# Experts of a mixture of experts: rows turned by VectorE instead of TensorE, four upward banks, downward products three chunks behind

## The chip, the cores and the metric

The kernel runs on one core of a Trainium2 chip. The metric is device time in microseconds (us) of one execution: before the change 3318.99 us, the median of three runs (3316.73 to 3319.85).

## The reference

`x` is [8, 1024, 256], 8192 tokens of width 256. The block is a "macaron":

```
x = x + 0.5 * moe(layernorm(x))
x = x + rwkv6_attention(layernorm(x))
x = x + 0.5 * moe(layernorm(x))          # same expert weights

moe: logits = x @ router_w.T + router_b;  top 2 of 16 experts;  gates = softmax
     each expert takes at most 1280 of its tokens, in order; the rest is dropped
     h   = gelu(packed @ w1[e] + b1[e])     # 1280x256 @ 256x1024
     out = h @ w2[e] + b2[e]                # 1280x1024 @ 1024x256
     every token gets the gated sum of its experts' rows
```

The change touches the two expert stages alone (the line `h`, the line `out` and the gated sum).

## The kernel before, in words

Five stages run one after the other: constants, route a, experts a, attention with the second routing, experts b. A routing stage scatters each token's row into `slots` in DRAM, 260 floats a row: 256 of data and 4 of "tail" (token number, expert of its first choice, two gates). The stage `experts` (from L442) then takes the 16 experts in order.

One expert is 3 blocks of rows, `SIZES` = 512, 512 and 256 (L455). A block is 8 chunks (`FC`), a chunk being 128 of the 1024 hidden features; so an expert has 24 chunks, `c` counts them on, and `b`, `f` below are block and chunk in the block. A unit is 256 rows: units 0, 1 are block 0, units 2, 3 block 1, unit 4 block 2. All products are in three passes of a high and a low part (fp32r), so every operand is split: high by a cast, low by a subtraction.

The engines work through lists written out by hand, in order, and meet at semaphores:

- SP (`sp`, L539) loads weights in four parts per expert through two staging tiles, the rows of each unit (`load`, L547, one DMA of 256 runs of 1040 bytes) and the bias.
- TensorE (`pe`, L597): `up(c)` is 6 matmuls into a bank `pH` and `down(c)` is 4 pairs of matmuls (2 pairs in block 2) into `pO`, accumulated over the 8 chunks of a block. The loop (L659) does `up(c)`, then `down(c - LAG)`, with `LAG` = 2. After chunks f = 2 and 4 it turns one unit of the next block into `pT` (`turn`, L598, four 128x128 transposes). `up(c)` waits until the activations of `c - 2` have emptied its bank (two banks). `down` of the first chunk of a block waits until VectorE has taken the previous block's results out of the banks that it will overwrite (`out_ready`, L646).
- ScalarE (L677): two Gelu activations of each chunk, one into `h32`, one rounded into `hT` high.
- VectorE (L780): `split_h(c)` (L807) makes the low part of the activations; `out(m)` (L814) takes a unit's result out of `pO` in two instructions and signals `out_ready`; `split_x(m)` (L786) takes the turned rows out of `pT` into high and low parts, then gates and token numbers; `weights_low` makes the low part of a quarter of the next expert's weights. In the loop (L848) `out` of both units of the last block stands at f = 1, ahead of `split_h`; `split_x` stands at f = 3 and 5; `weights_low` at block 0, f = 4 and 7 and block 1, f = 4 and 7.
- GpSimd (L695): `weights_high` and, for each unit, `send`: scale by the gates and two indirect accumulating DMAs into `acc`. In stage b the last expert is added by VectorE instead (`fetch`, `merge`, `write`).

Of the kernel before, what the change touches and what calls it, by code (L numbers as in the profile page):

```python
# [6 lines left out]
U32 = mybir.dt.uint32  # L7
# [4 lines left out]
P = 128  # L12
# [429 lines left out]
def experts(nc, S, tag):  # L442

    with ExitStack() as ctx:
# [15 lines left out]
        LAG = 2  # L460
# [6 lines left out]
        xp = [sb(f"xp{m}", [P, 2, ROW]) for m in range(UNITS)]  # L467
# [16 lines left out]
        xp_loaded = [sem(f"xp_loaded{m}") for m in range(UNITS)]  # L484
# [22 lines left out]
        xp_d = S.slots[tag].rearrange("(n q p) d -> n p q d", p=P, q=2)  # L507
# [29 lines left out]
        with nc.Block() as block:  # L537
            @block.sync
            def _(sp):  # L539
                def weights(i, u, k):  # L540
                    if due(part(i, u, k)):
                        sp.wait_ge(w_split[k % 2], part(i, u, k))
                    e = i * 2 + u
                    src = w1_d[e][:, k, :] if k < 2 else w2_d[e][:, (k - 2) * 4:(k - 1) * 4, :]
                    sp.dma_start(staged(k), src).then_inc(w_loaded[k % 2], 16)

                def load(i, u, m):  # L547
                    n = i * NU + (u * UNITS + m)
                    if due(n - UNITS + 1):
                        sp.wait_ge(xp_free, n - UNITS + 1)  # L550
                    sp.dma_start(xp[m][:, :, :], xp_d[n]).then_inc(xp_loaded[m], 16)
# [8 lines left out]
                for m in range(2):  # L560
                    load(0, 0, m)
                for k in range(2, 4):
                    weights(0, 0, k)
                for m in range(2, UNITS):
                    load(0, 0, m)
                bias(0, 0)
                for m in range(2):
                    load(0, 1, m)

                def step(i, first, last):  # L570
                    for u in range(2):
                        if not (last and u == 1):
                            i1, u1 = (i, 1) if u == 0 else (i + 1, 0)
                            weights(i1, u1, 0)
                            bias(i1, u1)
                            for m in units(1):
                                load(i1, u1, m)
                            weights(i1, u1, 1)
                            weights(i1, u1, 2)
                            for m in units(2):  # L580
                                load(i1, u1, m)
                            weights(i1, u1, 3)
                        if not last:
                            for m in units(0):
                                load(i + 1, u, m)

                loop_with_ends(sp, E // 2, step)
                if END:
                    for m in range(UNITS):
                        sp.wait_ge(stored[m], (E - 1) * 32)  # L590
                    n = T // PARTS
                    for j in range(PARTS):
                        sp.dma_start(S.out[j * n:(j + 1) * n, :], S.acc[tag][j * n:(j + 1) * n, :]).then_inc(copied, 16)
                    sp.wait_ge(copied, PARTS * 16)

            @block.tensor
            def _(pe):  # L597
                def turn(i, u, m):  # L598
                    n = u * UNITS + m
                    pe.wait_ge(xp_loaded[m], i * 32 + (u * 16 + 16))  # L600
                    if due(i * NU + n - 1):
                        pe.wait_ge(xT_ready, i * NU + n - 1)
                    for q in range(2):
                        for k in range(DC):
                            t = pe.transpose(pT[n % 2][:, k, q * P:(q + 1) * P], xp[m][:, q, k * P:(k + 1) * P],  # L605
                                             S.ident[:, :])
                    t.then_inc(turned, 1)

                passes = [(HI, HI), (HI, LO), (LO, HI)]

                def up(i, c):
                    u, b, f = place(c)
                    if f == 0:
                        pe.wait_ge(xT_ready, i * NU + (u * UNITS + units(b)[-1] + 1))
                        if b == 0:
                            for k in range(2):
                                pe.wait_ge(w_split[k], part(i, u, k) + 1)
                    if due(i * NCH + c - 1):
                        pe.wait_ge(gelu_done, i * NCH + c - 1)
                    n = 0  # L620
                    for k in range(DC):
                        for a, z in passes:
                            t = pe.matmul(pH[c % 2][:, 0:SIZES[b]], w1[u][a][:, k, f * P:(f + 1) * P],  # L623
                                          xT[(u * BLOCKS + b) % 2][z][:, k, 0:SIZES[b]],
                                          start=(n == 0), stop=(n == 3 * DC - 1))
                            n += 1
                    t.then_inc(up_full, 1)

                def emptied(u, b, j):

                    m = 2 * b + j
                    if b == 0:
                        return u * UNITS - 1 - j
                    return u * UNITS + m - 2

                def down(i, c):
# [7 lines left out]
                    for q in range(SIZES[b] // P):  # L644
# [3 lines left out]
                        pe.matmul(pO[:, q, :], hT[s][HI][:, ts], w2[u][:, f, :, :].rearrange("p s d -> p (s d)"),  # L648
                                  start=(f == 0), stop=(f == FC - 1), skip_group_check=True)
                        t = pe.matmul(pO[:, q, 0:D], hT[s][LO][:, ts], w2[u][:, f, HI, :],  # L650
# [4 lines left out]

                for m in units(0):
                    turn(0, 0, m)

                def step(i, first, last):  # L659
                    for c in range(NCH):  # L660
# [4 lines left out]
                        u1, b1, over = after(u, b)  # L665
                        if f in (2, 4) and not (over and last):
                            j = f // 2 - 1
                            if j < len(units(b1)):
                                turn(i + 1 if over else i, u1, units(b1)[j])
# [7 lines left out]
            def _(act):  # L677
                def step(i, first, last):
                    for c in range(NCH):
# [7 lines left out]
                        for dst in (h32[c % 2], hT[c % SLOTS][HI]):  # L687
                            t = act.activation(dst[:, 0:SIZES[b]], pH[c % 2][:, 0:SIZES[b]], ACT.Gelu,  # L688
                                               bias=S.b1[:, bass.ds(i * (2 * FC) + (u * FC + f), 1)])
# [5 lines left out]
            def _(pool):  # L695
# [47 lines left out]
                def step(i, first, last):  # L743
                    for u in range(2):
# [10 lines left out]
                        more = not (last and u == 1)  # L755
                        if not (first and u == 0):
                            send(i if u else i - 1, 1 - u, UNITS - 1)
                        if more:
                            if due(i * NCH + u * CH):
                                pool.wait_ge(chunk_down, i * NCH + u * CH)  # L760
                            for k in range(2):
# [3 lines left out]
                        if more:  # L765
                            for k in range(2, 4):
                                weights_high(i1, u1, k)
# [12 lines left out]
            def _(dve):  # L780
# [5 lines left out]
                def split_x(i, u, m):  # L786
# [3 lines left out]
                    ts = slice(m % 2 * BS, m % 2 * BS + BS)  # L790
                    dve.wait_ge(turned, i * NU + n + 1)
# [4 lines left out]
                    dve.tensor_tensor(xT[r][LO][:, :, ts], pT[n % 2][:, :, :], xT[r][HI][:, :, ts],  # L796
                                      ALU.subtract).then_inc(xT_ready, 1)
                    if due(n + i * NU - UNITS + 1):
                        dve.wait_ge(stored[m], i * 64 + u * 32)
                    dve.scalar_tensor_tensor(out=gate[m][:, :], in0=xp[m][:, :, FIRST],  # L800
                                             scalar=S.iota_f[:, bass.ds(i * 2 + u, 1)], in1=xp[m][:, :, GATE01],
                                             op0=ALU.is_equal, op1=ALU.mult).then_inc(gate_part, 1)
                    dve.tensor_copy(to[m][:, :], xp[m][:, :, TOKEN].bitcast(U32))
                    dve.wait_ge(gate_part, i * NU + n + 1)
                    dve.tensor_tensor(gate[m][:, :], gate[m][:, :], xp[m][:, :, GATE1], ALU.add).then_inc(xp_free, 1)
# [8 lines left out]
                def out(i, u, m):  # L814
# [10 lines left out]
                    banks = slice(2 * (m % 2), 2 * (m % 2) + 2)  # L825
                    dve.tensor_tensor(ob[m][:, :, :], pO[:, banks, D:2 * D],  # L826
                                      b2[u][:, :].unsqueeze(1).to_broadcast([P, 2, D]), ALU.add).then_inc(out_part, 1)
                    dve.wait_ge(out_part, n + 1)
                    dve.tensor_tensor(ob[m][:, :, :], pO[:, banks, 0:D], ob[m][:, :, :],  # L829
# [17 lines left out]

                def step(i, first, last):  # L848
                    for c in range(NCH):
                        u, b, f = place(c)  # L850
                        if f == 1 and not (first and c < FC):
                            u0, b0, _ = place(c - FC)
                            for m in units(b0):
# [3 lines left out]
                        split_h(i, c)  # L857
# [5 lines left out]
                        if b < 2 and f in (4, 7) and not (last and u == 1):  # L863
                            weights_low(i if u == 0 else i + 1, 1 - u, 2 * b + f // 7)
# [1269 lines left out]
```

## Time and profile before

| | |
|---|---|
| median of three runs | 3318.99 us |
| the profiled execution | 3325.69 us, its span 3323.9 us |
| TensorE matmuls busy over the span | 2899.8 us, 87% |
| VectorE, ScalarE, GpSimd busy | 60%, 40%, 51% |
| experts a, experts b (first to last own instruction) | 295.7 to 1289.6 us, 2309.8 to 3316.3 us |
| DMA queue of SP, share of 16 engines | 20.3% |

A timeline row gives start, duration, engine, line, operation, output <- inputs, and in brackets how long the engine had been idle and what ended it. PE is TensorE's matmuls, DVE VectorE, ACT ScalarE, POOL GpSimd, SPq the sync engine's queue. A matmul's listed duration overlaps the next one's; its cost on the engine is the distance from its start to the next start.

### The profile page before, as it was taken

The numbers are of one execution on the slowest core, as the hardware profiler recorded it, in microseconds if no ns is written. First come the engines' busy times: TensorE is split into PE (matmuls) and PEld (weight loads), VectorE is DVE, ScalarE is ACT, GpSimd is POOL, SyncE is SP. The second block draws the span as 40 slices with busy tenths as digits, with TensorE's granted clock in tenths as the row PEclk, the third lists the DMA queues.
The fourth block names the chain that finished last, engine by engine and source line by source line (L and its number), as shares of the span: only waits on it lengthen the run. The fifth ranks groups of instructions, "written<-read, shape, count | busy, mean of one in ns | idle before, by whom it ended". The sixth has DMA issues, their size and how long they took to land. (4 is left out here: it accounts for less than half of the span.)

```text
span 3323.9 us, 63196 instructions
## 1 busy us (share of the span) xinstructions
PE 2899.8 (87%) x22656; PEld 2337.1 (70%) x22656; DVE 2005.2 (60%) x4425; ACT 1337.9 (40%) x2281; POOL 1695.3 (51%) x1510
## 2 busy tenths in 40 slices
PE   4453999999999995899999999974999999999997
PEld 4453888888888883466756666664888888888886
DVE  4343555555555653577888888753555555565563
ACT  3341444444444442343444444421444444444442
POOL 2543554554545443356676767644345445454543
PEclk9999999999999997899999999965999999999998
DMA  9813333343333324601111111002333334334334
GB/s 305 285 67 103 75 81 81 74 86 78 76 83 87 77 51 115 208 15 37 35 48 34 47 34 47 27 31 94 78 76 82 81 73 86 84 72 88 81 66 136
DMA packets 231849, 281.02 MB, mean 85 GB/s; under 512 B 18999, under 2 KB 214651, under 8 KB 231520
## 3 DMA queue, kind: packets, MB, share of 16 engines
q1 hardware_dynamic: 173760, 203.16, 20.3%
q0 software_dynamic: 57888, 75.16, 12.9%
q8 instruction: 130, 2.13, 0.3%
q14 instruction: 71, 0.58, 0.1%
HBM read 142.44 MB, written 146.41 MB: 87 GB/s over the span
## 5 line engine op out<-in xcount | busy, mean ns | idle before, releaser
L688 ACT ACTIVATE be_h<-be_pH,b 128x512 f32<-128x512 f32 (+1 forms) x384 | 237.2, 618 | 555.5 <-PE be_pH L623 483.1
L688 ACT ACTIVATE ae_h<-ae_pH,b 128x512 f32<-128x512 f32 (+1 forms) x384 | 237.2, 618 | 539.8 <-PE ae_pH L623 487.8
L714 POOL DMA_INDIRECT acc_a<-ae_ob,ae_to x160 | 254.9, 1593 | 94.1 <-POOL ae_ob L706 66.7
L706 POOL TENSOR_SCALAR ae_ob<-ae_ob,ae_gate 128x256 f32<-128x256 f32 x160 | 174.3, 1191 | 247.5 <-DVE ae_ob L829 247.5
L714 POOL DMA_INDIRECT acc_b<-be_ob,be_to x150 | 238.4, 1589 | 88.2 <-POOL be_ob L706 62.3
L706 POOL TENSOR_SCALAR be_ob<-be_ob,be_gate 128x256 f32<-128x256 f32 x150 | 163.0, 1183 | 222.4 <-DVE be_ob L829 222.4
L1461 POOL TENSOR_TENSOR m_xf<-m_tmp,m_xT 128x512 f32<-128x512 f32 x160 | 181.3, 1159 | 119.3 <-DVE m_tmp L1182 119.1
L434 POOL DMA_INDIRECT slots_a<-ar_row,ar_sidx x128 | 125.9, 984 | 158.7 <-issue 150.3
L1514 POOL DMA_INDIRECT slots_b<-m_row,m_sidx x128 | 152.9, 1195 | 84.0 <-issue 84.0
L1756 PEld LDWEIGHTS m_PP<-m_RP,m_KS 64*64 64x64 f32 x6656 | 121.1, 139 | 88.4 <-issue 87.3
L1756 PE MATMUL m_PP<-m_RP,m_KS 64*64 64x64 f32 x6656 | 135.7, 226 | 37.6 <-DVE m_A L1212 36.5
L811 DVE TENSOR_TENSOR ae_hT3l<-ae_h,ae_hT3h 128x512 fp32r<-128x512 f32 (+1 forms) x96 | 58.1, 605 | 162.1 <-ACT ae_hT3h L688 160.5
L811 DVE TENSOR_TENSOR be_hT3l<-be_h,be_hT3h 128x512 fp32r<-128x512 f32 (+1 forms) x96 | 58.1, 605 | 159.7 <-ACT be_hT3h L688 158.2
L1225 DVE TENSOR_TENSOR m_RP<-m_RP,m_tot 128x512 f32<-128x512 f32 x96 | 95.6, 996 | 80.9 <-PE m_PP L1756 80.9
L648 PE MATMUL be_pO<-be_w,be_hT1h 128*128 128x512 f32 x320 | 119.9, 405 | 22.2 <-DVE be_hT1l L811 22.2
L1182 DVE SCALAR_TENSOR_TENSOR m_tmp<-m_B,m_ch,m_xx 128x512 f32<-128x512 f32 x160 | 112.0, 741 | 44.6 <-PE m_B L1846 37.2
L648 PE MATMUL ae_pO<-ae_w,ae_hT1h 128*128 128x512 f32 x320 | 118.7, 402 | 16.3 <-DVE ae_hT1l L811 16.2
L648 PE MATMUL be_pO<-be_w,be_hT0h 128*128 128x512 f32 x320 | 122.5, 411 | 11.9 <-DVE be_ob L829 10.9
L648 PE MATMUL ae_pO<-ae_w,ae_hT0h 128*128 128x512 f32 x320 | 121.9, 409 | 8.3 <-DVE ae_ob L829 7.4
L648 PE MATMUL be_pO<-be_w,be_hT2h 128*128 128x512 f32 x320 | 117.6, 397 | 0.0
L648 PE MATMUL be_pO<-be_w,be_hT3h 128*128 128x512 f32 x320 | 117.0, 396 | 0.2 <-DVE be_hT3l L811 0.2
L648 PE MATMUL ae_pO<-ae_w,ae_hT3h 128*128 128x512 f32 x320 | 116.9, 396 | 0.2 <-DVE ae_hT3l L811 0.2
(342 smaller groups left out, 9384.7 us busy)
## 6 DMA issues: line engine op xcount, KB each, us to landing
ae_stage<-in_w SPq DMA_DIRECT2D x64, 512.0 KB
be_stage<-in_w SPq DMA_DIRECT2D x64, 512.0 KB
slots_a<-empty SPq DMA_DIRECT2D x10, 2080.0 KB, 19.7
ae_xp<-slots_a SPq DMA_DIRECT2D x80, 260.0 KB
slots_b<-empty SPq DMA_DIRECT2D x10, 2080.0 KB, 19.2
be_xp<-slots_b SPq DMA_DIRECT2D x80, 260.0 KB
ar_xin<-in_x SPq DMA_DIRECT2D x16, 512.0 KB, 5.8
acc_a<-ar_xin SPq DMA_DIRECT2D x16, 512.0 KB
```

The lines of the kernel that those rows point to most:

```text
L434: pool.indirect_dma_start(S.slots[tag][:, :], bass.IndirectOffsetOnAxis(ap=sidx[u][:, q, k:k + 1], axis=0), row[u][:, q, :], None, bounds_ ...
L648: pe.matmul(pO[:, q, :], hT[s][HI][:, ts], w2[u][:, f, :, :].rearrange("p s d -> p (s d)"), start=(f == 0), stop=(f == FC - 1), skip_group ...
L688: t = act.activation(dst[:, 0:SIZES[b]], pH[c % 2][:, 0:SIZES[b]], ACT.Gelu, bias=S.b1[:, bass.ds(i * (2 * FC) + (u * FC + f), 1)])
L706: t = pool.tensor_scalar(ob[m][:, q, :], ob[m][:, q, :], gate[m][:, q:q + 1], None, ALU.mult)
L714: pool.indirect_dma_start(S.acc[tag][:, :], bass.IndirectOffsetOnAxis(ap=to[m][:, q:q + 1], axis=0), ob[m][:, q, :], None, bounds_check=T ...
L811: dve.tensor_tensor(hT[s][LO][:, 0:SIZES[b]], h32[c % 2][:, 0:SIZES[b]], hT[s][HI][:, 0:SIZES[b]], ALU.subtract).then_inc(h_split, 1)
L1182: drains(dve.scalar_tensor_tensor(out=tmp[m % TMP][:, :], in0=bank(f"M{m}", g)[:, :], scalar=ch[:, 1 + f, k:k + 1], in1=xx[:, k, :], op0=A ...
L1225: dve.tensor_tensor(rp[:, :, 1, :], rp[:, :, 1, :], pieces(l)[:, :, 0:1].to_broadcast([P, DC * GT >> (l + 1), 1 << l]), ALU.mult).then_inc ...
L1461: pool.tensor_tensor(xf[f][:, k, :], tmp[m % TMP][:, :], xT[g % 2][:, k, 1:GT + 1], ALU.add).then_inc(mixed, 1)
L1514: pool.indirect_dma_start(S.slots["b"][:, :], bass.IndirectOffsetOnAxis(ap=sidx[w][:, q, k:k + 1], axis=0), row[w][:, q, :], None, bounds_ ...
L1756: t = pe.matmul(PP[c * N:c * N + N, h, to], ks[rows, r, ts], rp[rows, r, ss], start=True, stop=True, skip_group_check=True)
```

## The change

What it does, part by part:

1. TensorE's `turn` goes, and the banks `pT` with it. SP loads a block's rows so that each partition group j of 32 holds, for features 32j to 32j + 31 of each half, blocks of 32 rows by 32 features (`xq`): 8 DMAs per block, 24 per expert, of 128-byte runs. VectorE turns a unit with one `transpose` of 32x32 blocks (128x512) into `x32`, then casts and subtracts from there. The tails come by one DMA per expert.
2. `LAG` is 3, and `up` has four banks `pH`.
3. `pO` is two tiles of two banks. Units 0, 2, 4 have the first (`HOME` 0), units 1, 3 the second.
4. VectorE: `split_h` comes first in each step; `out` of the even unit at f = 2, of the odd one at f = 3, each behind `split_h` of that chunk. `weights_low` moves to block 0, f = 2, 4, 7 and block 1, f = 4.
5. SP issues both first weight parts of the next expert ahead of its rows; at the very start the rows of block 0 go first. GpSimd makes the next expert's first two high parts as soon as the last `up` of the expert before is done, ahead of `send` of its unit 4, and the other two right behind that `send`.

```diff
-        LAG = 2
+        LAG = 3
-        pT = [ps(f"pT{r}", [P, DC, BS]) for r in range(2)]
-        pH = [ps(f"pH{r}", [P, FULL]) for r in range(2)]
-        pO = ps("pO", [P, 4, 2 * D])
+        UPS = 4
+        pH = [ps(f"pH{r}", [P, FULL]) for r in range(UPS)]
+        pO = [ps(f"pO{r}", [P, 2, 2 * D]) for r in range(2)]
+        HOME = (0, 1, 0, 1, 0)
...
+                def load(i, u, b):
+                    m = units(b)[-1]
+                    if due(i * NU + (u - 1) * UNITS + m + 1):
+                        sp.wait_ge(xp_free, i * NU + ((u - 1) * UNITS + m + 1))
+                    e = i * 2 + u
+                    n0, n1 = b * FULL // BLK, (b * FULL + SIZES[b]) // BLK
+                    for j in range(QUADS):
+                        for k in range(DC):
+                            cs = slice(k * P + j * BLK, k * P + j * BLK + BLK)
+                            sp.dma_start(xq[b][j * BLK:(j + 1) * BLK, k, :].rearrange("i (n d) -> i n d", d=BLK),
+                                         x_d[e][:, n0:n1, cs]).then_inc(xq_loaded[b], 16)
...
+                load(0, 0, 0)
                 for k in range(2):
                     weights(0, 0, k)
...
-                            weights(i1, u1, 0)
+                            for k in range(2):
+                                weights(i1, u1, k)
+                            load(i1, u1, 0)
+                            load_tails(i1, u1)
                             bias(i1, u1)
...
+                            for k in range(2, 4):
+                                weights(i1, u1, k)
+                            load(i1, u1, 1)
+                            load(i1, u1, 2)
...
-                    if due(i * NCH + c - 1):
-                        pe.wait_ge(gelu_done, i * NCH + c - 1)
+                    if due(i * NCH + c - UPS + 1):
+                        pe.wait_ge(gelu_done, i * NCH + c - UPS + 1)
...
                     m = 2 * b + j
-                    if b == 0:
-                        return u * UNITS - 1 - j
-                    return u * UNITS + m - 2
+                    before = [k for k in range(m) if HOME[k] == HOME[m]]
+                    if before:
+                        return u * UNITS + before[-1]
+                    return (u - 1) * UNITS + [k for k in range(UNITS) if HOME[k] == HOME[m]][-1]
...
+                    dve.transpose(x32[n % 2][:, :, :], xq[b][:, :, ts]).then_inc(turned, 1)
                     dve.wait_ge(turned, i * NU + n + 1)
-                    dve.tensor_copy(xT[r][HI][:, :, ts], pT[n % 2][:, :, :]).then_inc(xT_high, 1)
+                    dve.tensor_copy(xT[r][HI][:, :, ts], x32[n % 2][:, :, :]).then_inc(xT_high, 1)
...
+                LOWS = [(0, 2), (0, 4), (0, 7), (1, 4)]
...
-                        if f == 1 and not (first and c < FC):
+                        split_h(i, c)
+                        if f in (2, 3) and not (first and c < FC):
                             u0, b0, _ = place(c - FC)
-                            for m in units(b0):
+                            for m in units(b0)[f - 2:f - 1]:
                                 out(i if c >= FC else i - 1, u0, m)
...
-                        split_h(i, c)
```

## Rows read from the trace of the kernel before

**Rows 1.** The page: granted clock in tenths and GB/s, in 40 slices.

```profile
PEclk9999999999999997899999999965999999999998
GB/s 305 285 67 103 75 81 81 74 86 78 76 83 87 77 51 115 208 15 37 35 48 34 47 34 47 27 31 94 78 76 82 81 73 86 84 72 88 81 66 136
```

**Rows 2.** Windows view, experts a: length, busy per engine (instructions), clock, DMA share, GB/s.

```profile
309.00:1281.00 972.00, 946.97 (x5164) 802.03 (x5164) 561.59 (x993) 430.50 (x766) 467.00 (x375) 1.00 0.36 76
```

**Rows 3.** Waits of TensorE, 309 to 1281: total us, times, longest.

```profile
PE ae_pO L648 <- DVE ae_hT1l L811: 16.2, 15, 1.7
PE ae_pO L648 <- DVE ae_ob L829: 7.4, 34, 0.3
PE ae_pH L623 <- ACT ae_hT0h L688: 0.4, 1, 0.4
```

**Rows 4.** Timeline, TensorE: the same place in two experts that follow each other.

```profile
532.37 0.50 PE L648 MATMUL ae_pO<-ae_w,ae_hT1h 128*128 128x512 f32 x1 [0.98 <-DVE ae_hT1l L811]
...
593.38 0.50 PE L648 MATMUL ae_pO<-ae_w,ae_hT1h 128*128 128x512 f32 x1 [0.98 <-DVE ae_hT1l L811]
```

**Rows 5.** Timeline at a change of block, 512-row chunks.

```profile
513.47 0.39 PE L623 MATMUL ae_pH<-ae_xT0h,ae_w_1l 128*128 128x512 f32 x1
513.70 0.40 PE L648 MATMUL ae_pO<-ae_w,ae_hT3h 128*128 128x512 f32 x1
...
513.99 0.69 ACT L688 ACTIVATE ae_h<-ae_pH,b 128x512 f32<-128x512 f32 x1 [1.53 <-PE ae_pH L623]
...
514.58 0.68 ACT L688 ACTIVATE ae_hT1h<-ae_pH,b 128x512 fp32r<-128x512 f32 x1
514.60 0.69 DVE L826 TENSOR_TENSOR ae_ob<-ae_pO,ae_b 128x512 f32<-128x512 f32 x1 [0.53 <-PE ae_pO L650]
...
515.11 0.40 PE L623 MATMUL ae_pH<-ae_xT0h,ae_w_1h 128*128 128x512 f32 x1
515.33 0.69 DVE L829 TENSOR_TENSOR ae_ob<-ae_pO,ae_ob 128x512 f32<-128x512 f32 x1
...
515.94 0.68 DVE L826 TENSOR_TENSOR ae_ob<-ae_pO,ae_b 128x512 f32<-128x512 f32 x1
...
517.39 0.50 PE L648 MATMUL ae_pO<-ae_w,ae_hT0h 128*128 128x512 f32 x1
```

**Rows 6.** Timeline in the 256-row block, with one turn and one `split_x`.

```profile
542.29 0.43 DVE L811 TENSOR_TENSOR ae_hT3l<-ae_h,ae_hT3h 128x256 fp32r<-128x256 f32 x1 [1.04 <-ACT ae_hT3h L688]
...
542.42 0.28 PE L623 MATMUL ae_pH<-ae_xT1h,ae_w_1l 128*128 128x256 f32 x1
...
542.63 0.68 DVE L794 CAST ae_xT0h<-ae_pT 128x512 fp32r<-128x512 f32 x1
...
542.83 0.48 ACT L688 ACTIVATE ae_h<-ae_pH,b 128x256 f32<-128x256 f32 x1 [0.57 <-PE ae_pH L623]
...
543.20 0.47 ACT L688 ACTIVATE ae_hT0h<-ae_pH,b 128x256 fp32r<-128x256 f32 x1
543.24 0.60 PE L605 MATMUL ae_pT<-ident,ae_xp 128*128 128x128 f32 x4
...
544.62 0.42 DVE L811 TENSOR_TENSOR ae_hT0l<-ae_h,ae_hT0h 128x256 fp32r<-128x256 f32 x1
```

**Rows 7.** Timeline, SP's queue at the start of experts a.

```profile
293.18 0.94 SPq L551 DMA_DIRECT2D ae_xp<-slots_a  x2
```

**Rows 8.** Waits of TensorE in the last expert of experts b, 3262 to 3302.

```profile
PE be_pO L648 <- DVE be_hT1l L811: 6.1, 2, 4.0
PE be_pO L648 <- DVE be_ob L829: 3.9, 2, 3.8
```

**Rows 9.** Windows view: behind the 2.0 us wait of rows 8, and around a 1.6 us wait.

```profile
3301.60:3304.90 3.30, 3.30 (x16) 3.11 (x15) 0.85 (x2) 0.84 (x2) 1.75 (x2) 0.50 0.33 119
2728.00:2732.00 4.00, 2.39 (x13) 1.67 (x12) 3.24 (x3) 1.06 (x2) 1.05 (x2) 1.00 0.16 25
```

**Rows 10.** DMA view, 1303.7 to 1305.1: strips of 128-byte runs loaded for attention.

```profile
DMA packets 1868, 0.28 MB, mean 202 GB/s; under 512 B 1792, under 2 KB 1868, under 8 KB 1868
```

More of the change, by code:

```diff
@@ L466, in experts @@
         b2 = [sb(f"b2_{u}", [P, D]) for u in range(2)]
-        xp = [sb(f"xp{m}", [P, 2, ROW]) for m in range(UNITS)]
+        xq = [sb(f"xq{b}", [P, DC, SIZES[b]]) for b in range(BLOCKS)]
+        tails = [sb(f"tails{u}", [P, 2 * UNITS, ROW - D]) for u in range(2)]
+        x32 = [sb(f"x32_{r}", [P, DC, BS]) for r in range(2)]
         xT = [[sb(f"xT{r}{k}", [P, DC, FULL], F32R) for k in "hl"] for r in range(2)]
@@ L483, in experts @@
         b2_loaded = [sem(f"b2_loaded{u}") for u in range(2)]
-        xp_loaded = [sem(f"xp_loaded{m}") for m in range(UNITS)]
+        xq_loaded = [sem(f"xq_loaded{b}") for b in range(BLOCKS)]
+        tails_loaded = [sem(f"tails_loaded{u}") for u in range(2)]
         stored = [sem(f"stored{m}") for m in range(UNITS)]
@@ L556, in bias @@
                     sp.dma_start(b2[u][:, :], S.b2[i * 2 + u].partition_broadcast(P)).then_inc(b2_loaded[u], 16)
+                load(0, 0, 0)
                 for k in range(2):
                     weights(0, 0, k)
[L560 to L561 removed]
+                load_tails(0, 0)
                 for k in range(2, 4):
                     weights(0, 0, k)
[L564 to L565 removed]
+                load(0, 0, 1)
                 bias(0, 0)
[L567 to L568 removed]
+                load(0, 0, 2)
                 def step(i, first, last):
@@ L597, in _ @@
             def _(pe):
[L598 to L607, printed above, removed]
                 passes = [(HI, HI), (HI, LO), (LO, HI)]
@@ L664, in step @@
                             down(i, c - LAG)
[L665 to L669, printed above, removed]
                     if last:
@@ L755, in step @@
                         more = not (last and u == 1)
+                        if more:
+                            if due(i * NCH + u * CH):
+                                pool.wait_ge(up_full, i * NCH + u * CH)
+                            for k in range(2):
+                                weights_high(i1, u1, k)
                         if not (first and u == 0):
@@ L760, in step @@
                                 pool.wait_ge(chunk_down, i * NCH + u * CH)
-                            for k in range(2):
+                            for k in range(2, 4):
                                 weights_high(i1, u1, k)
@@ L764, in step @@
                             send(i, u, m)
-                        if more:
-                            for k in range(2, 4):
-                                weights_high(i1, u1, k)
                         for m in units(1):
@@ L862, in step @@
                                 split_x(i + 1 if over else i, u1, units(b1)[j])
-                        if b < 2 and f in (4, 7) and not (last and u == 1):
-                            weights_low(i if u == 0 else i + 1, 1 - u, 2 * b + f // 7)
+                        if (b, f) in LOWS and not (last and u == 1):
+                            weights_low(i if u == 0 else i + 1, 1 - u, LOWS.index((b, f)))
                     if last:
```

57 lines of the change are left out of this document (27 added, 30 removed).

## The prediction

> **What bounds the kernel now.** I read the page first, then the windows of an expert stage, TensorE's waits, and last the timeline of one expert. The page's clock is at full speed in both expert stages [rows 1]. In experts a the matmuls are busy 947 of 972 us, VectorE 562, ScalarE 431, GpSimd 467 [rows 2]: TensorE is the bound, and only its own work or its own waits can move the time. Its waits are short: 16.2 us behind `split_h`, 7.4 us behind `out`, and 0.4 us in one wait for an upward bank [rows 3]. The last says that two more `pH` banks have nothing to remove by themselves.
>
> One expert lasts 61.01 us, the distance of the same matmul in two experts [rows 4]. Of that the products need: an `up` matmul 0.23 us, six are 1.40; a `down` of four pairs 513.70 to 515.11, 1.41 [rows 5]. A full chunk is 2.81 us, one of 256 rows half of it, 1.405. So 16 x 2.81 + 8 x 1.405 = 56.2 us. The other 4.8 us of each expert are five turns and the waits. That is all the change can take away: 32 experts x 4.8 = 154 us.
>
> **What goes.** All turns and, as the steps below put them elsewhere, all the old waits: -4.8 us an expert. The longest of these (0.98 us) stands in both experts at the same place, where `split_h` comes late [rows 4]; with `LAG` 3 `down(c)` runs one chunk later, 2.8 us more of slack, so that kind goes.
>
> **What comes: VectorE's `out` behind `split_h`.** This is the step that decides. `down(8)`, the first of block 1, overwrites the banks of units 0 and 1, so it needs `out(0)` for its first half and `out(1)` for its second. TensorE's order is now up(10), down(7), up(11), down(8). VectorE's is split_h(10), out(0), split_h(11), out(1). So `out(1)` cannot start before up(11) has gone through ScalarE and `split_h`, and down(8) stands right behind up(11). The length of that chain, from the start of the last `up` matmul: 0.52 to the first activation, 0.59 to the second, 0.68 for it, 0.61 for `split_h` (a VectorE instruction of this size frees the engine after 0.61, 515.33 to 515.94), 0.73 and 0.69 for the two of `out`, 0.03 to the matmul: 3.85 us [rows 5]. Without a wait TensorE would be there sooner. At each block change:
>
> - A, block 2 to the next expert's block 0: needs `out(4)`, behind split_h(f=2). TensorE comes after 0.23 + 0.70 (down, 256 rows) + 1.40 (up) = 2.34. Wait 1.51 us.
> - B, block 0 to 1: first half after 0.23 + 1.41 + 1.40 = 3.04, wait 0.81 for `out(0)`; second half, from up(11), after 0.23 + 0.71 = 0.94, so the two waits together are 3.85 - 0.94 = 2.91 us, the second 2.10.
> - C, block 1 to 2, 256-row chunks: the chain is 0.41 + 0.37 + 0.47 [rows 6] + 0.34 + 1.42 + 0.03 = 3.04, where 0.34 is 542.29 to 542.63. TensorE comes after 0.12 + 1.41 + 0.70 = 2.23. Wait 0.81 us.
>
> Before, both `out` stood at f = 1 ahead of `split_h`; those waits were at most 0.3 us [rows 3]. The chain has only latencies in it; while it runs nothing else on TensorE can go first.
>
> **D, the turned rows.** VectorE now also turns. The trace has no such instruction. The nearest row is the cast of the same 128x512 from `pT`: 0.68 us long, 0.72 to an instruction that waits for it, as between L826 and L829 (514.60 to 515.33) [rows 5]; I take 0.72. Below, it could be half, 0.36; above, 1.0. `split_x` took 542.63 to 544.62, 1.99 us [rows 6], and becomes 2.71. In block 2 two of them stand at f = 3 and 5 between short chunks. Counted from the last `up` matmul of f = 2: out(2) ends 2.93; split_h(f=3) waits for its activation and ends 3.70; out(3) 5.04; split_x(0) 7.75; two split_h 8.43; transpose, cast, subtraction: rows ready for TensorE at 8.43 + 0.72 + 0.72 + 0.72 = 10.59. TensorE, after the wait of C at 3.04, does down 0.81, then four ups and four downs, 5.64: it wants them at 9.48. Wait 1.1 us. With halves for transpose and cast it is 0; with 1.0 for the transpose 1.7.
>
> The Trainium skill says ("VectorE: DVE Perf Modes", section "The perf-mode tier table") that a one-source copy of fp32 from SBUF runs at twice the rate that a PSUM source allows. No row here has such a copy. By it the two casts of D would give back about 0.5 us an expert, 16 us in all, which stays inside the range.
>
> A matmul behind a wait lasts 0.50 instead of 0.40 [rows 4, 5]: five waits, 0.5 us. Sum an expert: 1.51 + 2.91 + 0.81 + 1.1 + 0.5 = 6.8 us new against 4.8 old, +2.0. Over 32 experts +65; A and D don't occur before a stage's first expert, -5.
>
> **Start of a stage.** Eight DMAs of rows stand ahead of the first weights. Two issues take 0.94 us [rows 7], so eight take 3.8, and the weights come that much later; two transposes add 1.4 before the first `up`. 2 x 5.2 = +10 us.
>
> **The last expert of stage b** waits twice, 3.8 and 4.0 us, for the fetched sums [rows 8]. `fetch` follows the send of unit 4, which is a chunk later now, but a late `merge` holds down(12) only three chunks on instead of two. I take half away: -4.
>
> **Clock.** After the wait of 2.0 us (the smaller of the 6.1 in two [rows 8]) TensorE ran at 1.2 GHz (granted 0.50) for 3.3 us; around a 1.6 us wait it stayed at 2.4 GHz (1.00) [rows 9]. B has 0.8 and 2.1 us within 4. If every B ended so, 3.3 us at half speed cost 1.65 us each, 32 x 1.65 = 53; if none, 0. B lies just beyond the row that fell; I take 30.
>
> **Costed at nothing.** SP has 30 issues an expert instead of 10, 30 x 0.47 = 14 of 61 us, and its waits are for buffers freed an expert earlier. Loads of the next rows are issued about 24 chunks before use. The 128-byte runs: 10,240 an expert. 1868 packets passed in 1.4 us [rows 10], 0.75 ns each, so 7.7 us an expert. `weights_high` has the time from the last `up` to f = 2. `weights_low` at f = 4 and 7 is covered by three chunks of lag; without the cover it would be the old wait of 1 us. GpSimd's and the DMA queues' order isn't on TensorE's path: TensorE never waited for weights [rows 3].
>
> **Sum**: +65 - 5 + 10 - 4 + 30 = +96 us. On the profiled execution 3325.7 + 96 = 3422; that execution was 6.7 us above the median, so on the median 3319 + 96 = 3415 us.
>
> **Rivals.**
>
> 1. Faster. The waits A to C don't bind: if VectorE reaches `out` before TensorE reaches the banks, as before, the 4.8 us of turns and waits go and only short waits as in rows 3 remain (0.3 x 4 an expert). Then -154 + 38 + 10 = about 3213 us. It decides where `out(1)` is ready within 0.94 us of the last `up` matmul of f = 3. For it: VectorE is idle 40% of the stage. Against: idle time does not help a list worked in order, and `split_h(11)` needs `up(11)`. Chance 0.08, and 0.03 more for half waits that cancel to within 0.2%.
> 2. Short runs make DMA the bound. At 0.75 ns this is far off. It decides from about 6 ns a packet. The Trainium skill says ("DMA: Bandwidth & Descriptors", section "Rules for kernel authors") that a plain DMA with a rearranged access pattern is 19 times slower than a hardware transpose. As a mechanism here: an expert's 1.33 MB at the page's best slice, 305 GB/s [rows 1], is 4.4 us; 19 times that is 83 us, more than the expert's 63. Then each expert lasts 83 us, +22 x 32: 4020 us. The strips of rows 10 are the same kind of run and passed at 202 GB/s, so 0.03.
> 3. The clock falls at every B, and the transpose takes 1.0 us: +23 and +17, 3455 us. Chance 0.12.
> 4. The change removes waits that are not there: "weights first" and the four banks. TensorE waited for neither, so this is part of my forecast.
>
> **Numbers.** Forecast as summed 0.74. Its own range: without D and without the clock -63, with rival 3 +40, and a few us for rounding: 3350 to 3458. This also holds 8 in 10 overall, since only rivals 1 and 2 lie outside. 0.2% (6.6 us) is about what a measurement of this kernel can tell from none. Faster 0.09, same 0.03, slower 0.88.
>
> **What would show it.** In the trace after: no L605; waits of `pO` matmuls for `ob` of 1.5, 0.8 + 2.1 and 0.8 us an expert, over 150 us in all; waits of `pH` matmuls for `xT` near 1 us; the period of an expert 63 to 64 us; stretches of granted clock 0.5 in the expert stages. I am wrong if the waits for `ob` stay near 0.3 us, if the period falls under 61, or if TensorE waits for `xq`.

## The result, and the profile after

The changed kernel takes 3484.5 us (median of 4, 3482.8 to 3487.4), the kernel before 3319.4 us (4 runs, 3316.7 to 3320.6): ratio 1.0498 [1.0484, 1.0513], 165 us slower. Forecast were 3415 us with a range to 3458. The direction was right, the size 70 us short.

The page of the changed kernel: busy times, granted clock in tenths, DMA packets.

```profile
PE 2901.2 (83%) x22016; PEld 2325.8 (67%) x22016; DVE 2132.3 (61%) x4585; ACT 1337.6 (38%) x2281; POOL 1783.2 (51%) x1510
PEclk9999999999999998799999999866999999999999
DMA packets 569771, 281.06 MB, mean 81 GB/s; under 512 B 397879, under 2 KB 552571, under 8 KB 569440
```

The windows view from the first `up` of experts a to their last matmul, before and after (columns as in [rows 2]):

```profile
303.20:1280.80 977.60, 952.39 (x5176) 805.99 (x5176) 564.23 (x997) 433.27 (x769) 467.85 (x376) 1.00 0.36 77
301.30:1365.60 1064.30, 957.22 (x4864) 802.97 (x4864) 631.87 (x1075) 433.11 (x769) 510.23 (x375) 0.96 0.40 70
```

TensorE executes fewer matmuls (x4864 against x5176, the turns are gone), is busy 5 us longer all the same, and the stage is 87 us longer; the clock over the stage is 0.96 where it was 1.00. So it waits, and part of its work runs slower. The profiled executions (3325.7 us before, 3487.4 after) differ by 161.7 us:

| Stretch | before | after | difference |
|---|---|---|---|
| up to SP's first issue of experts a | 292.3 | 283.5 | -8.9 |
| from there to the first `up` | 10.9 | 17.9 | +7.0 |
| first `up` to last matmul, experts a | 977.6 | 1064.3 | +86.6 |
| between the two expert stages | 1025.6 | 1029.4 | +3.7 |
| start of experts b | 10.9 | 18.2 | +7.3 |
| first `up` to last matmul, experts b | 993.3 | 1059.3 | +65.9 |

The first row is work that the change does not touch, and I leave it unexplained. The bodies hold 152.5 of the 161.7 us. The period of one expert went from 61.05 to 66.6 us; forecast were 63.0 and about 1 for the clock.

TensorE's waits, 312 to 1370 (total us, times, longest), the answer to [rows 3]:

```profile
PE ae_pO L653 <- DVE ae_ob L834: 93.6, 63, 3.0
PE ae_pH L626 <- DVE ae_xT1l L800: 7.4, 8, 1.0
PE ae_pH L626 <- DVE ae_xT0l L800: 6.0, 7, 1.0
```

The 16.2 us behind `split_h` are gone, as forecast. The 7.4 us behind `out` (34 times, at most 0.3) became 93.6 us, up to 3.0 each, and the turned rows cost 13.4. Sorted by place over both stages, all from the timeline:

| Wait | times | us in all | each | forecast each |
|---|---|---|---|---|
| A, next expert's block 0 | 30 | 81.8 | 2.73 | 1.51 |
| B, block 1, two waits | 32 pairs | 84.6 | 0.71 + 1.82 | 0.81 + 2.10 |
| C, block 2 | 32 | 23.5 | 0.7 | 0.81 |
| D, turned rows | 30 | 27 | 0.9 | 1.1 |

B, C and D are as predicted within 0.4 us. A is not.

The timeline of the changed kernel at an A and at the B behind it (start, length, engine and line, idle time before it in brackets), and the order of VectorE at each:

```profile
571.07 3.26 DVE L817 TENSOR_TENSOR ae_hT1l<-ae_h,ae_hT1h 128x512 fp32r<-128x512 f32 x1 [1.41 <-issue]
571.17 2.60 POOL L696 CAST ae_w_1h<-ae_stage 128x1024 fp32r<-128x1024 f32 x2
...
572.42 0.68 ACT L685 ACTIVATE ae_hT2h<-ae_pH,b 128x512 fp32r<-128x512 f32 x1
...
574.25 0.68 DVE L817 TENSOR_TENSOR ae_hT2l<-ae_h,ae_hT2h 128x512 fp32r<-128x512 f32 x1
574.85 0.68 DVE L831 TENSOR_TENSOR ae_ob<-ae_pO,ae_b 128x512 f32<-128x512 f32 x1
575.57 0.69 DVE L834 TENSOR_TENSOR ae_ob<-ae_pO,ae_ob 128x512 f32<-128x512 f32 x1
576.40 0.47 PE L653 MATMUL ae_pO<-ae_w,ae_hT0h 128*128 128x512 f32 x1 [2.69 <-DVE ae_ob L834]
...
597.58 0.69 DVE L817 TENSOR_TENSOR ae_hT2l<-ae_h,ae_hT2h 128x512 fp32r<-128x512 f32 x1 [2.09 <-ACT ae_hT2h L685]
...
599.65 0.50 PE L653 MATMUL ae_pO<-ae_w,ae_hT0h 128*128 128x512 f32 x1 [0.71 <-DVE ae_ob L834]
600.37 0.69 DVE L817 TENSOR_TENSOR ae_hT3l<-ae_h,ae_hT3h 128x512 fp32r<-128x512 f32 x1 [0.78 <-ACT ae_hT3h L685]
600.98 0.68 DVE L831 TENSOR_TENSOR ae_ob<-ae_pO,ae_b 128x512 f32<-128x512 f32 x1
...
602.30 0.70 DVE L794 STREAM_TRANSPOSE ae_x<-ae_xq 128x512 f32<-128x512 f32 x1
602.44 0.55 PE L653 MATMUL ae_pO<-ae_w,ae_hT0h 128*128 128x512 f32 x1 [1.82 <-DVE ae_ob L834]
603.04 0.43 DVE L798 CAST ae_xT0h<-ae_x 128x512 fp32r<-128x512 f32 x1
604.07 0.63 PE L626 MATMUL ae_pH<-ae_xT1l,ae_w_0h 128*128 128x512 f32 x1
604.50 0.63 PE L626 MATMUL ae_pH<-ae_xT1h,ae_w_0l 128*128 128x512 f32 x1
```

B is the forecast chain: `out` stands behind a `split_h` that waits for its activation. At A, `split_h` of f = 1 lasts 3.26 us instead of 0.69. It runs beside GpSimd's first two casts of the next weights, 571.17 to 573.77, which the change moved there, and ends 0.56 us after the second. The activation that `split_h` of f = 2 needs ends at 573.10, but `split_h` starts only at 574.25: 1.15 us late, and the wait is 2.69 instead of 1.51, 1.18 more. In the whole trace 28 of the 512 `split_h` of this width overlap both casts of a pair and last 3.26 to 3.58 us; all 67 that overlap a cast average 2.26 us, and of the other 445, with a mean of 0.69, none lasts over 0.92. The Trainium skill states a mechanism ("SBUF — State Buffer", section "Who interferes with whom"): a VectorE instruction with two inputs in SBUF contends with a GpSimd instruction that reads SBUF. The trace agrees, with 0.69 against 2.26 us. But overlap alone is not enough: in `e10` below 91 `split_h` overlap a cast and average 0.82 us, none over 1.58. What makes the difference was not separated.

Behind B the matmuls of one product start 0.43 us apart, 604.07 to 604.50, not 0.23. The windows view of B's two waits and of the stretch behind them, the answer to [rows 9]:

```profile
596.00:602.70 6.70, 4.17 (x20) 3.02 (x19) 4.28 (x7) 2.54 (x4) 2.05 (x2) 1.00 0.00 0
602.80:606.10 3.30, 3.30 (x10) 2.72 (x9) 1.65 (x6) 0.00 (x0) 3.00 (x3) 0.50 0.39 42
```

TensorE goes from 2.4 GHz (1.00) to 1.2 GHz (0.50) behind the pair of waits. This happened behind 31 of the 32 B (109 us at 1.2 GHz) and behind 14 of the 30 A (58 us). Half of these 167 us, 83, is lost, since a matmul takes 0.43 us there and not 0.23.

The lines view of VectorE, 312 to 1370 (busy us, mean ns, idle before):

```profile
L817 DVE TENSOR_TENSOR ae_hT1l<-ae_h,ae_hT1h 128x512 fp32r<-128x512 f32 x63 | 90.4, 1434 | 88.7 <-ACT ae_hT1h L685 76.6 <-issue 12.1
L794 DVE STREAM_TRANSPOSE ae_x<-ae_xq 128x512 f32<-128x512 f32 x78 | 54.7, 702 | 0.0
L798 DVE CAST ae_xT1h<-ae_x 128x512 fp32r<-128x512 f32 x40 | 19.9, 498 | 1.4
```

The turn of 128x512 takes 0.70 us (0.72 was assumed). `split_h` into `hT1l`, the one beside the casts, has a mean of 1.43.

### The profile page after: what moved, and what is told of

It reads as the page before. It is cut to its first block and busy times, and to the rows that moved or that the text cites. A ratio compares the mean times of both kernels' runs of the same rounds, so it can differ in the third digit from the quotient of the medians.

```text
span 3485.6 us, 63656 instructions
## 1 busy us (share of the span) xinstructions
PE 2901.2 (83%) x22016; PEld 2325.8 (67%) x22016; DVE 2132.3 (61%) x4585; ACT 1337.6 (38%) x2281; POOL 1783.2 (51%) x1510
## 2 busy tenths in 40 slices
DMA packets 569771, 281.06 MB, mean 81 GB/s; under 512 B 397879, under 2 KB 552571, under 8 KB 569440
## 5 line engine op out<-in xcount | busy, mean ns | idle before, releaser
L703 POOL TENSOR_SCALAR ae_ob<-ae_ob,ae_gate 128x256 f32<-128x256 f32 x160 | 210.6, 1464 | 400.0 <-DVE ae_ob L834 400.0
L703 POOL TENSOR_SCALAR be_ob<-be_ob,be_gate 128x256 f32<-128x256 f32 x150 | 199.8, 1489 | 370.5 <-DVE be_ob L834 370.5
L653 PE MATMUL ae_pO<-ae_w,ae_hT0h 128*128 128x512 f32 x320 | 130.3, 433 | 93.6 <-DVE ae_ob L834 93.6
L1763 PEld LDWEIGHTS m_PP<-m_RP,m_KS 64*64 64x64 f32 x6656 | 121.4, 139 | 85.7 <-issue 84.6
L817 DVE TENSOR_TENSOR be_hT1l<-be_h,be_hT1h 128x512 fp32r<-128x512 f32 (+1 forms) x96 | 108.0, 1125 | 114.9 <-ACT be_hT1h L685 103.4
L817 DVE TENSOR_TENSOR ae_hT1l<-ae_h,ae_hT1h 128x512 fp32r<-128x512 f32 (+1 forms) x96 | 104.6, 1090 | 117.2 <-ACT ae_hT1h L685 105.1
L653 PEld LDWEIGHTS be_pO<-be_w,be_hT0h 128*128 128x128 f32 x320 | 62.2, 194 | 128.8 <-DVE be_ob L834 59.3
L817 DVE TENSOR_TENSOR ae_hT0l<-ae_h,ae_hT0h 128x512 fp32r<-128x512 f32 (+1 forms) x96 | 63.7, 664 | 136.5 <-ACT ae_hT0h L685 130.1
L653 PEld LDWEIGHTS ae_pO<-ae_w,ae_hT0h 128*128 128x128 f32 x320 | 62.8, 196 | 126.3 <-DVE ae_ob L834 58.5
L1232 DVE TENSOR_TENSOR m_RP<-m_RP,m_tot 128x512 f32<-128x512 f32 x96 | 85.4, 890 | 91.7 <-PE m_PP L1763 91.6
L817 DVE TENSOR_TENSOR be_hT0l<-be_h,be_hT0h 128x512 fp32r<-128x512 f32 (+1 forms) x96 | 58.2, 607 | 128.6 <-ACT be_hT0h L685 121.4
L626 PE MATMUL ae_pH<-ae_xT0h,ae_w_0h 128*128 128x512 f32 (+1 forms) x256 | 88.9, 347 | 55.4 <-DVE ae_xT0l L800 55.4
```

The source lines that it names most:

```text
L626: t = pe.matmul(pH[c % UPS][:, 0:SIZES[b]], w1[u][a][:, k, f * P:(f + 1) * P], xT[(u * BLOCKS + b) % 2][z][:, k, 0:SIZES[b]], start=(n == ...
L653: pe.matmul(to[:, q % 2, :], hT[s][HI][:, ts], w2[u][:, f, :, :].rearrange("p s d -> p (s d)"), start=(f == 0), stop=(f == FC - 1), skip_g ...
L703: t = pool.tensor_scalar(ob[m][:, q, :], ob[m][:, q, :], gate[m][:, q:q + 1], None, ALU.mult)
L817: dve.tensor_tensor(hT[s][LO][:, 0:SIZES[b]], h32[c % 2][:, 0:SIZES[b]], hT[s][HI][:, 0:SIZES[b]], ALU.subtract).then_inc(h_split, 1)
L1763: t = pe.matmul(PP[c * N:c * N + N, h, to], ks[rows, r, ts], rp[rows, r, ss], start=True, stop=True, skip_group_check=True)
```

## The experiments

Every kernel was timed in three rounds beside the kernel before, on the same chip. `e1`, `e3`, `e4` and `e5` ran where the kernel before took 3318.6 us; `e2`, `e6`, `e7` and `e8` ran on a second chip, where it took 3273.2 us, and `e9` to `e12` on a third, where it took 3272.4. So only ratios to the kernel before are compared, and a gain in us is such a ratio times 3319.

### e1: both `out` first

```diff
 # after, VectorE's list
-split_h(i, c)
-if f in (2, 3) and not (first and c < FC):
+if f == LAG - 1 and not (first and c < FC):
     u0, b0, _ = place(c - FC)
-    for m in units(b0)[f - 2:f - 1]:
+    for m in units(b0):
         out(i if c >= FC else i - 1, u0, m)
+split_h(i, c)
```

> The kernel after with one thing moved on VectorE: both out of the last block stand at f = 2 ahead of split_h, as before they stood at f = 1 with a lag of two. Theory 1 (the time was lost because out(1) stands behind split_h of a chunk whose up is right ahead of the down that needs it; the clock fell behind those waits): the waits of pO matmuls for ob shrink from about 190 us to under 20 us, the stretches at 1.2 GHz inside the expert stages (168 us) nearly go, an expert takes about 58 us in place of 66.5, and the time is 3200 to 3240 us, under the kernel before too. Rival (the loads in 128-byte runs or the transposes on VectorE cost the time): these stay, so it stays above 3400 us.

1.0050 [1.0032, 1.0067], 3333.3 us: it gives back most of the loss, but not what was expected. B's and C's waits are gone, so the order of `out` made them. A stays, 2.1 to 2.4 us in 28 of 30 places, with 75 us at 1.2 GHz behind it. The waits of TensorE for `ob` in `e1`, 312 to 1170:

```profile
PE ae_pO L653 <- DVE ae_ob L834: 28.9, 15, 2.4
```

Fifteen waits, one an expert at most. This is the part that order alone does not explain.

### e2: GpSimd's casts at their old places

```diff
 # after, GpSimd's step: send of unit 4, then casts 0 and 1; sends of block 0, then casts 2 and 3
-LOWS = [(0, 2), (0, 4), (0, 7), (1, 4)]
+LOWS = [(0, 4), (0, 7), (1, 4), (1, 7)]
```

> The kernel after with only GpSimd's casts and VectorE's weights_low back at their old places; out stays behind split_h. Theory: the wait at block 2 to 0 falls from 2.7 to the 1.5 us that the chain of latencies gives, the clock falls at block 0 to 1 alone: 30 x 1.2 plus half of the 58 us of slow clock behind it, 3484 - 65 = 3420 us. Rival (the casts do not matter): 3475 to 3490 us.

1.0389 [1.0372, 1.0406], which is 0.990 of the changed kernel's ratio, some 36 us, where 65 were expected. `out` stays behind `split_h`. A falls to 1.59 us in all 30 places, against the 1.51 of the forecast, and no `split_h` lasts over 1.5 us. B and C stay. So the early casts, and not the order of `out`, made the rest of A. At 1.2 GHz there are 65 us instead of 167: the same pair of waits at B now drops the clock 12 times of 32, not 31. But a wait of 1.4 us for `split_h` comes back at chunk 13 (block 1, f = 5, the place of [rows 4]), 19 times over the two stages, 28 us in all, the second group here (TensorE, 312 to 1170):

```profile
PE ae_pO L653 <- DVE ae_ob L832: 63.8, 53, 1.8
PE ae_pO L653 <- DVE ae_hT1l L815: 12.1, 8, 2.1
```

### e3: only the turning on VectorE and SP's order

`LAG` and `UPS` are 2, both `out` first, casts and `LOWS` as in `e2`.

> Rows by block turned by VectorE, and SP's new order, alone: lag 2, two upward banks, both out at f = 1 ahead of split_h, GpSimd's and weights_low's places as in the kernel before. Theory 1: TensorE's five turns (about 2.2 us an expert) go, a wait for the turned rows of under 1 us comes; 3250 to 3300 us. Rival (loads and transposes cost): at or above 3400 us, as the kernel after.

1.0099 [1.0081, 1.0117], against an expectation of no more than 0.995. TensorE's turns are gone, but the old wait for `split_h` at chunk 13 grew from 0.98 us [rows 4] to 2.1:

```profile
PE ae_pO L653 <- DVE ae_hT1l L815: 34.3, 26, 3.4
```

Just ahead of that `split_h` VectorE waits for a cast of GpSimd in `weights_low`, in the kernel before (L783) and in `e3` (L780):

```profile
529.68 2.03 DVE L783 TENSOR_TENSOR ae_w<-ae_stage,ae_w 128x1024 fp32r<-128x1024 f32 x1 [4.57 <-POOL ae_w L699]
530.79 2.04 DVE L780 TENSOR_TENSOR ae_w<-ae_stage,ae_w 128x1024 fp32r<-128x1024 f32 x1 [5.00 <-POOL ae_w L696]
```

So VectorE has time to spare there; it is GpSimd that comes 1.1 us later against TensorE's arrival. Its `send` ahead of the casts scales for 3.1 us where it took 2.4, and starts later. TensorE also waits 12 times in a stage, 0.5 us each, for one of its two upward banks.

### e4: only the order and the banks

The kernel before with `LAG` 3, four output banks by `HOME`, and `out` behind `split_h` at f = 2 and 3. TensorE turns.

> The kernel before with the order alone: lag 3, out of the even unit at f = 2 and of the odd one at f = 3, each behind split_h, pO in two homes; turns stay on TensorE, two upward banks, loads as before. Theory 1: the waits of 1.5 to 2.8, 0.7 + 1.8 and 0.7 us come as in the kernel after, and the clock falls behind them; about the kernel after plus the turns less the wait for turned rows: 3480 to 3540 us. Rival (loads and transposes cost): near the kernel before, 3300 to 3360 us.

1.0381 [1.0363, 1.0399], 3443.5 us. B is 0.34 + 2.43 us, C 0.34, A 1.13, and 120 us of the two stages run at 1.2 GHz. It came out below the expected 3480, but 125 us on the slow side, far from the rival: three quarters of the loss come without VectorE's turns. `e4` has no wait at chunk 13. Against `e9` below, which has the same lag with `out` first (1.0045), the order of `out` and its banks cost 3.3%, some 110 us.

### e5: keeping TensorE busy in its waits

```diff
 # after, before the waits of A and of B's second half; the products land in a free upward bank and are thrown away
+def fill(i, c):
+    pe.wait_ge(gelu_done, i * NCH + c - UPS + 1)
+    for r in range(FILL):        # 16
+        pe.transpose(pH[c % UPS][:, 0:P], S.ones[:, :], S.ident[:, :])
```

> The kernel after with 16 transposes of constants (about 1.75 us of TensorE work that is thrown away) ahead of two of its waits: down's second half at block 0 to 1 and down's first half at the next expert's block 0. If the clock falls because TensorE stands still there, the stretches at 1.2 GHz (92 and 76 us in the two expert stages) go, each giving back half its length: 84 us less, about 3400 us, while out_ready comes no earlier. If the clock is not what these waits cost, the time stays within 10 us of 3484 or rises by the filling.

1.0295 [1.0274, 1.0317], 3416.1 us, 68 us less than the changed kernel, with nothing else changed. No stretch at 1.2 GHz begins in the two stages. The windows view of experts a, clock 1.00 where it was 0.96:

```profile
303.00:1325.00 1022.00, 970.41 (x5360) 827.22 (x5360) 642.71 (x1075) 432.56 (x769) 525.20 (x375) 1.00 0.42 73
```

Of the 83 us that the clock cost, 68 came back. The chains behind the waits remain; the thrown-away products fill part of them (36 us of waiting for `ob` are left of experts a's 94). This measures the clock's term apart from the waits, rather too low than too high, since the filling adds work.

### e6: the same rows in long runs

```diff
 # after, SP's load of rows: as many DMAs and bytes; an expert's rows are other numbers
-x_d[e][:, n0:n1, cs]          # runs of 128 bytes
+xl_d[e][rows, units, 0:D]     # runs of 1024 bytes
```

> The kernel after with the rows loaded in 1024-byte runs in the same number of DMAs and bytes; VectorE turns what lies there, so the expert inputs are other numbers. If the 128-byte runs cost anything, the time falls from 3484 us by that; my theory says within 10 us of 3484 and the same waits of TensorE. Rival (the loads slow the stage): 50 us less or more.

Packets under 512 bytes fall from 397,879 to 70,196. 1.0512 [1.0492, 1.0531] against 1.0498 [1.0484, 1.0513]: the intervals overlap. No cost of the short runs shows, as forecast. The 19-fold rule of the Trainium skill ("DMA: Bandwidth & Descriptors", section "Rules for kernel authors") that the prediction weighed does not decide this kernel's time.

### e7 and e8: the casts later, then the rows earlier

```diff
 # e7 = e1 with the casts and LOWS of e2
 # e8 = e7 with this in VectorE's list
-if f in (3, 5) and not (over and last):
+turns = (1, 4) if b == BLOCKS - 1 else (3, 5)
+if f in turns and not (over and last):
```

> As the run with out first, and GpSimd's casts of the next weights' high parts and VectorE's weights_low back at their old places: casts behind send of unit 4, weights_low at block 0, f = 4, 7 and block 1, f = 4, 7. Theory: the wait of 2.1 to 2.7 us at block 2 to 0 is there because the two early casts on GpSimd (2.6 us) run beside split_h(f=1), which then takes 3.3 us in place of 0.7 and holds back split_h(f=2) and out(4). With them later that wait is about 0.3 us, the clock falls at few places: 3333 - 32 x (1.8 + 1.1) = 3240 us. Rival (that wait is the lag's or the bank's, not the casts'): it stays near 2.1 us and the time within 15 us of 3333.

> As e7_casts_later, and in block 2 the two split_x stand at f = 1 and 4 in place of 3 and 5. Theory (the wait of 1.0 us for the turned rows at an expert's first up is VectorE's list in the short chunks of block 2): it goes, 30 x 1.0 us less than e7_casts_later, about 3210 us. Rival (the rows' DMA or the transposes' own length): the wait stays.

e7: 1.0089 [1.0068, 1.0110]; e8: 1.0066 [1.0049, 1.0083]. Both missed: 0.976 and less were expected. In `e7` A is down to 0.2 to 0.3, but a wait of 2.14 us stands at chunk 13. Timeline of `e7` there:

```profile
547.01 2.60 POOL L696 CAST ae_w<-ae_stage 128x1024 fp32r<-128x1024 f32 x2
...
548.66 2.04 DVE L780 TENSOR_TENSOR ae_w<-ae_stage,ae_w 128x1024 fp32r<-128x1024 f32 x1 [7.48 <-POOL ae_w L696]
...
551.36 0.50 PE L653 MATMUL ae_pO<-ae_w,ae_hT1h 128*128 128x512 f32 x1 [2.14 <-DVE ae_hT1l L815]
```

`weights_low` waits 7.48 us for a cast that is now late, with all of VectorE's list behind it. Three chunks of lag do not cover that. So the casts can be too late as well as too early; I had moved a wait, not removed it. In `e8` the wait for turned rows went, but one of about 0.8 us for `ob` came between blocks 1 and 2, since `split_x` now stands ahead of `out` in VectorE's list.

### e9: only the lag, from the kernel before

```diff
-LAG = 2
+LAG = 3
-if f == 1 and not (first and c < FC):
+if f == LAG - 1 and not (first and c < FC):
```

> The kernel before with two edits: lag 3, and both out at f = 2 (still ahead of split_h). TensorE turns, two upward banks, GpSimd and weights_low as before. Theory: the one long wait of before (1.0 us an expert for split_h behind weights_low and casts) is covered by the third chunk of lag unless VectorE is held up longer; 0.985 to 0.995 of before. Rival: GpSimd's casts come a chunk later behind out and sends, VectorE waits longer for them, and the gain is eaten: 1.00.

1.0045 [1.0030, 1.0059]. The rival was right. More lag removes no wait here: `send`, and so the casts behind it, start a chunk later, and the wait at chunk 13 grows from 0.98 to 2.13 us.

```profile
PE ae_pO L648 <- DVE ae_hT1l L811: 33.7, 15, 3.0
```

### e10 and e11: the casts early, but behind `out`

```diff
 # e10 = e1 with this in GpSimd's step, ahead of the first two casts
+if not (first and u == 0):
+    pool.wait_ge(out_ready, i * NU + u * UNITS)
 # and in VectorE's list
-LOWS = [(0, 2), (0, 4), (0, 7), (1, 4)]
+LOWS = [(0, 3), (0, 4), (0, 7), (1, 4)]
 # e11 = e10 with turns = (2, 4) for block 2, as in e8
```

> As the run with out first (both out at f = 2 ahead of split_h, 3333 us on its chip, 1.005 of before), and GpSimd's first two casts wait until out of unit 4 is taken, still ahead of its send; weights_low at block 0, f = 3, 4, 7 and block 1, f = 4. Theory (GpSimd's pair of casts beside split_h(f=1) delays out(4), and casts that come too late make VectorE wait in weights_low, as the run with the casts behind the sends showed): here neither happens, the wait at block 2 to 0 is about 0.3 us, none of 2 us is left, the clock hardly falls in the expert stages; 0.975 to 0.985 of before. Rival (a wait of 2 us moves on to another place whatever the order of GpSimd, since VectorE as a whole is short): 1.00 or more.

> As e10_casts_after_out, and in block 2 the split_x stand at f = 2 and 4 in place of 3 and 5. Theory (the 1.0 us for the turned rows at an expert's first up is VectorE's list in block 2): it falls to about 0.3 us without a new wait for out, 0.5% less than e10_casts_after_out. Rival: the wait stays, or one for ob of the same size comes, as with f = 1 and 4 (0.8 us there).

e10: 0.9775 [0.9758, 0.9792], inside the expected 0.975 to 0.985. Waiting for unit 4's `out` keeps GpSimd's first pair of casts off the `split_h` that A hangs on, and leaves them early enough for `weights_low`. The pair now runs beside a later `split_h`, which is not slowed:

```profile
501.75 2.58 POOL L696 CAST ae_w_1h<-ae_stage 128x1024 fp32r<-128x1024 f32 x2 [2.48 <-DVE ae_ob L836]
502.72 0.71 DVE L819 TENSOR_TENSOR ae_hT3l<-ae_h,ae_hT3h 128x512 fp32r<-128x512 f32 x1 [0.74 <-ACT ae_hT3h L685]
```

TensorE's waits in `e10`, 272 to 1170; D is left, and 0.2 to 0.3 us behind `out`:

```profile
PE ae_pH L626 <- DVE ae_xT0l L802: 7.4, 7, 1.1
PE ae_pH L626 <- DVE ae_xT1l L802: 7.2, 8, 1.0
PE ae_pO L653 <- DVE ae_ob L836: 4.5, 18, 0.3
```

No stretch of experts a is at 1.2 GHz; the period is 58.4 us. e11: 0.9759 [0.9742, 0.9775]. D falls from 0.97 to 0.64 us on average in experts a, but the two intervals overlap, so this step is not shown as a gain.

### e12: e10's order with the turns on TensorE

The kernel before with `LAG` 3, two upward banks, the old load of rows, both `out` first at f = 2, and GpSimd's wait, `LOWS` and SP's two weight loads first as in `e10`.

> The order of e10_casts_after_out (lag 3, both out first at f = 2, the casts behind out of unit 4, weights_low at the same places, both first weight parts ahead in SP's queue) on the kernel before: TensorE still turns, rows come in 1040-byte runs, two upward banks. Against e10 this tells what the turning on VectorE is worth: 2.2 us an expert more for TensorE, less the 1.0 us wait for the turned rows, so 1.2 us x 32 = 38 us, 1.1% of before above e10_casts_after_out. Rival (the turn on VectorE gains nothing since its waits eat it): equal to e10 within 0.3%.

0.9751 [0.9735, 0.9768]: as fast as `e10` and `e11`, where 1.1% more had been expected. TensorE has no wait of 0.2 us or more in experts a. Windows view of that stage of `e12`:

```profile
248.00:1190.00 942.00, 938.78 (x5184) 807.79 (x5184) 574.77 (x1005) 433.36 (x769) 499.10 (x377) 1.00 0.38 81
```

It is busy 938.8 of 942 us. Its period is also 58.4 us: the 56.2 of the products and 2.2 of turns. In `e10` these 2.2 are exchanged for D's wait, for 0.2 to 0.3 us behind `out` and for some 1.0 that I leave unexplained. The body of stage a is 3.2 us shorter in `e10`, and its start 7 us longer (17.9 against 10.9).

## Why the prediction was wrong

By steps, over both stages:

- **Order of `out`.** Right, and it decides. B came to 2.53 us for 2.91 (84.6 us in all for 93), C 23.5 us for 26. `e1` removes both; `e4` has them without the rest of the change.
- **A, and "Costed at nothing".** The failed step. The prediction said that GpSimd's order "isn't on TensorE's path" and that `weights_high` "has the time", and gave the casts no price. That TensorE never waits for weights [rows 3] was the wrong row to ask. The casts reach TensorE in another way: beside the pair the `split_h` that A hangs on lasts 3.3 us and more instead of 0.69, and `out(4)` stands behind it. A cost 81.8 us and not 45: 37 us missing. `e2` gives A back as 1.59, with the casts elsewhere; `e10` leaves 0.2 to 0.3 of it, with `out` first and the casts just behind it.
- **What goes.** The old wait for `split_h` went, but not for the reason given. The prediction let the third chunk of lag cover it; with that lag alone (`e9`) it grows from 0.98 to 2.13 us, and in `e2` it comes back. The early casts had removed it: luck. What they saved here they lost again at A and in the clock, and 36 us more (`e2`).
- **Clock.** The mechanism was right, the term mis-sized: 83 us for 30, so 53 missing. B dropped the clock 31 times of 32 and lost 54 us, the bound of 53 itself; A, which had no term here, lost 29. `e5` gave 68 us back by filling the waits. Part of this miss may hang on A as well: in `e2`, with A at 1.59 and B as before, 65 us at 1.2 GHz lost 32, near the 30 taken. Why the same B then drops the clock less often is not shown.
- **Turned rows.** D 27 us for 33; the turn 0.70 for 0.72. The cast took 0.43 where the one from `pT` took 0.68. The Trainium skill's rule ("VectorE: DVE Perf Modes", section "The perf-mode tier table"), which I had left out of the sum, points the right way, though the gain is less than twofold.
- **Start of stage.** 7.0 and 7.3 us for 5.2: a third short. Eight issues took 4.3 for 3.8.
- **Last expert of b.** It was 15.5 us longer than the last expert of a before (76.5 against 61.0) and is 3.1 longer after (69.0 against 65.9): 12 us gained, where 4 were forecast. The waits of 3.8 and 4.0 us of [rows 8] are gone; the longest wait for `ob` in this stage is 3.0. This miss hid part of the others.
- **Banks and runs.** Right: no wait for `pH`'s banks, nothing for the short runs (`e6`).

The two bodies grew by 152.5 us; the forecast had 86 for them (65 - 5 - 4 + 30). The waits (+20), the clock (+53) and the last expert (-8) make 65 of the 66 us between. The terms overlap by a few us (the last expert has its own B and its own drop of the clock), so the match is looser than it looks.

The upper end of 3458 was short because no term in it let VectorE be slowed by a neighbour, and because the clock was bounded by B alone. What the change was worth without its two faults is seen in `e10`: 0.9775 of before, 0.931 of the changed kernel. And `e12` shows that none of this comes from VectorE's turning; it comes with the lag of 3, `out` first and the casts right behind it. Lag and `out` first without that place of the casts give nothing (`e9`, `e1`, `e7`). Which of SP's order and `weights_low`'s places `e12` also needs was not separated, and whether the casts' new place would do with a lag of 2 was not run.

## What to carry to other kernels

In a list that an engine works in order, put what frees another engine's buffer ahead of what waits for that engine's newest product: here the other order cost some 110 us. When work on one engine is moved, look at what then runs beside it on the other engines, and not only at who waits for its result; an instruction of three to five times its usual length in the lines or the timeline is the sign. Short waits that come in pairs are paid as waits and again as clock; price both from rows at the lower clock, and try cheap filler work where the wait itself can't go.

## What the runs showed of the hardware

- Two GpSimd casts of 128x1024 from fp32 (2.60 us as a pair) raised a VectorE subtraction of 128x512 with both inputs in SBUF from 0.69 to 3.26 us: it began 0.10 us ahead of the pair and ended 0.56 us after the second cast. In `e10` such a subtraction ran in 0.71 us inside such a pair (2.58 us).
- A wait of 0.71 and one of 1.82 us, whose ends lie 2.8 us apart, dropped TensorE to 1.2 GHz 31 times of 32 in the changed kernel, but 12 of 32 in `e2`. Single waits at A did so 14 times of 30 at 1.6 to 3.0 us, 20 of 30 in `e1` at mostly 2.1 to 2.4, and never at 1.59 (`e2`). Sixteen thrown-away 128-column transposes ahead of A and of B's second wait held it at 2.4 GHz.
- With rows in runs of 1024 bytes instead of 128 the kernel took the same time, within what the two ratios allow (1.0512 and 1.0498, each known to 0.2%).
